# Second attention: where the gate is applied, and by which engine the projection is added to the rows

## The reference, cut to what matters

```
h = layernorm(x) * (1 + ca) + sa
Q, K, V = h @ Wq.T, h @ Wk.T, h @ Wv.T          # 16 heads of 16
scores = einsum('bshd,bstd->bsht', Q, K) / 4     # heads against heads, inside one token
attn = softmax(scores, axis=-1)
out = einsum('bsht,bstd->bshd', attn, V).reshape(b, s, dm)
x = x + ga * (out @ Wfc.T)                       # ga: one row of 256 per batch
h = layernorm(x) * (1 + cb) + sb                 # goes to the routed part
```

## Time and profile before

| what | value |
|---|---|
| median of 3 runs | 1049.5 us (1048.51 to 1049.79) |
| span of the profiled execution | 1045.7 us |
| second attention, first to last step | about 553 to 822 us of the span |
| busy over the span | PE 959.2 us, DVE 690.6 us, ACT 496.8 us, POOL 377.1 us |
| mean granted TensorE clock | 0.969 |

### The profile page before, as it was taken

One profiled execution on the slowest core, in us unless ns is written; L12 is line 12 of the kernel. 1 busy time (PEld: TensorE's weight loads), 2 busy tenths in 40 slices (PEclk: granted clock), 3 DMA queues, 4 the chain that ended last, 5 costly groups with the idle time before them and its releaser, 6 DMA issues. The chain is left out here.

```text
span 1045.7 us, 30362 instructions
## 1 busy us (share of the span) xinstructions
PE 959.2 (92%) x11177; PEld 823.6 (79%) x11178; DVE 690.6 (66%) x1747; ACT 496.8 (48%) x1343; POOL 377.1 (36%) x330
## 2 busy tenths in 40 slices
PE   6899999889999999999987999999767888999996
PEld 3466666879999999999965778888666878899995
DVE  3478877855777777777412688889985776344442
ACT  3556665404454554554446777777552440322221
POOL 0134335521223223222213455555561101455552
PEclk9999999999999999999998899999868999999998
DMA  9885581294232222221055657766421620444441
GB/s 338 216 331 122 126 269 41 97 386 115 85 102 79 87 97 85 89 92 71 8 107 92 115 124 150 154 134 128 99 68 57 266 108 22 151 134 140 134 136 35
DMA packets 133025, 135.59 MB, mean 130 GB/s; under 512 B 73884, under 2 KB 122142, under 8 KB 130740
## 3 DMA queue, kind: packets, MB, share of 16 engines
q1 hardware_dynamic: 121684, 90.80, 31.5%
q0 software_dynamic: 11232, 43.27, 13.0%
HBM read 96.21 MB, written 44.77 MB: 135 GB/s over the span
## 5 line engine op out<-in xcount | busy, mean ns | idle before, releaser
L1151 PE MATMUL psall<-rows 128*128 128x128 f32 x1872 | 224.8, 277 | 1.6 <-issue 1.1
L1151 PEld LDWEIGHTS psall<-rows 128*128 128x128 f32 x1872 | 219.6, 194 | 3.1 <-issue 1.3
L1114 POOL DMA_INDIRECT x<-ffn_rows,tok_i x78 | 82.6, 1059 | 171.8 <-DVE tok_i L999 69.9
L1165 PE MATMUL psall<-whi,rows 128*128 x624 | 141.0, 379 | 0.0
L1244 DVE COPY rows<-wlo 128x2048 f32 (+2 forms) x78 | 74.5, 955 | 95.8 <-PE psall L1151 85.2
L1165 PEld LDWEIGHTS psall<-whi,rows 128*128 128x128 f32 x624 | 115.7, 190 | 14.1
L1119 POOL DMA_INDIRECT attn_rows<-rows,tok_i x39 | 41.7, 1070 | 183.9 <-DVE rows L1276 183.9
L1504 DVE STREAM_TRANSPOSE whi<-whi 32x512 f32<-32x512 f32 x128 | 89.7, 701 | 9.1 <-POOL whi L1467 7.7
L1584 ACT ACTIVATE whi<-psall 32x512 f32<-32x512 f32 x128 | 75.3, 588 | 30.8 <-PE psall L1713 27.3
L280 PE MATMUL psall<-cst 128*128 128x128 f32 x714 | 88.4, 280 | 0.5 <-PEq L1387 0.5
L1306 ACT ACTIVATE rows<-psall,vs 128x128 f32<-128x128 f32 x312 | 85.0, 383 | 4.4 <-PE psall L1151 2.1
(11 more groups left out here) (250 smaller groups left out, 1731.3 us busy)
## 6 DMA issues: line engine op xcount, KB each, us to landing
ffn_rows<-mod_rows SPq DMA_DIRECT2D x2, 4096.0 KB
wlo<-in_W SPq DMA_DIRECT2D x2, 4096.0 KB, 17.5
whi<-in_w SPq DMA_DIRECT2D x5, 1024.0 KB
whi<-mod_rows SPq DMA_DIRECT2D x4, 1024.0 KB, 15.0
ffn_rows<-rows SPq DMA_DIRECT2D x8, 512.0 KB
ffn_rows<-x SPq DMA_DIRECT2D x8, 512.0 KB
wlo<-attn_rows SPq DMA_DIRECT2D x32, 128.0 KB, 3.4
v_turn<-wlo SPq DMA_DIRECT2D x32, 128.0 KB, 2.6
```

The costliest lines, as they stand in the source:

```text
L1114: eng.indirect_dma_start(xin[j % DEEP], None, src_d, bass.IndirectOffsetOnAxis(tok_i[:, j:j + 1].bitcast(U32), 0), bounds_check=T, oob_is_ ...
L1151: last = eng.matmul(b_up[t.par][f // 4][:, (f % 4) * P:(f % 4 + 1) * P], w_now[:, c, f * P:(f + 1) * P], inT[t.par][:, c * P:(c + 1) * P], ...
L1165: last = eng.matmul(b_dn[t.par][:, 0:D], hidT[t.par][:, f * P:(f + 1) * P], w_down[:, bass.ds(e, 1), f, :].rearrange("p o n -> p (o n)"), ...
```

## The change

The gate row is loaded by itself into one buffer (`gate_row`) at lag 14. GpSimd multiplies it into a copy of the projection's weights (`wfc_g`, 128x2048) in three parts of 768, 768 and 512 columns, in the first three of the four steps from lag 15 on, each at the end of GpSimd's list for that step. TensorE's projection reads `wfc_g` and waits for the third part. GpSimd's four additions per batch and VectorE's four gate multiplications are gone; VectorE adds the projection from PSUM to the rows of the whole batch in one instruction of 128x1024.

```diff
@@ constants and buffers
-        yb = cv(TB * D).rearrange("p (k d) -> p k d", d=D)
-        mod3 = [cw(3 * D).rearrange("p (j d) -> p j d", d=D) for _ in range(2)]
+        mod2 = [cw(2 * D).rearrange("p (j d) -> p j d", d=D) for _ in range(2)]
+        cx = Carve(x)
+        wfc_g = cx(HH * D).rearrange("p (j n) -> p j n", j=HH)
+        gate_row = cx(D)
+        b_y4 = psall[:, 0:TB * 512].rearrange("p (k n) -> p k n", k=TB)[:, :, 0:D]
@@ sync: layer_rows loads two rows, and
+                def load_gate(t):
+                    b = t // TB
+                    if t % TB == 0:
+                        eng.wait_ge(ev["pre"], 3 * B + b)
+                        eng.dma_start(gate_row, mod_d[b:b + 1, (6 + GA) * D:(7 + GA) * D].broadcast_to([P, D])).then_inc(s_wb, 16)
-                tile_steps([(0, load_norm), (LAG_VST, store_v), (LAG_VLD, load_v), (LAG_XLD, load_x), (LAG_ROW, layer_rows),
+                tile_steps([(0, load_norm), (LAG_VST, store_v), (LAG_VLD, load_v), (LAG_XLD, load_gate), (LAG_XLD, load_x), (LAG_ROW, layer_rows),
                             (LAG_H, store_rows), (LAG_QK, turn_k)])
@@ gpsimd
-                def add_attention(t):
-                    b, k = t // TB, t % TB
-                    eng.wait_ge(c_["ya"], b + 1)
-                    eng.wait_ge(s_x1[b % 2], 16 * (b // 2 + 1))
-                    eng.tensor_tensor(xr[b % 3][:, k, :], xr[b % 3][:, k, :], yb[:, k, :], ALU.add).then_inc(c_["xa"], 1)
-                tile_steps([(LAG_ET, normalize_exp), (LAG_X, add_attention), (LAG_MX, mask_other), (LAG_MX, sub_max)])
-                for t in LAST:
-                    add_attention(t)
+                def gate_weights(t):
+                    b, part = t // TB, t % TB
+                    if part == 0:
+                        eng.wait_ge(s_wa, 16 + 16 * (2 + TB))
+                        eng.wait_ge(s_wb, 48 + 16 * (b + 1))
+                        wait_some(eng, c_["y"], b)
+                    if part < 3:
+                        js = slice(3 * part, min(3 * part + 3, HH))
+                        last = eng.tensor_tensor(wfc_g[:, js], wfc[:, js], bc_mid(gate_row, js.stop - js.start), ALU.mult)
+                        if part == 2:
+                            last.then_inc(ev["pre"], 1)
+                tile_steps([(LAG_ET, normalize_exp), (LAG_MX, mask_other), (LAG_MX, sub_max), (LAG_Y, gate_weights)])
@@ vector
-                def gate_attention(t):
+                def add_attention(t):
                     b = t // TB
                     if t % TB == TB - 1:
                         eng.wait_ge(c_["y"], b + 1)
-                        eng.wait_ge(s_m3[b % 2], 48 * (b // 2 + 1))
-                        wait_some(eng, c_["xa"], TB * b)
-                        for k in range(TB):
-                            last = eng.tensor_tensor(yb[:, k, :], b_y[k], mod3[b % 2][:, 0, :], ALU.mult)
-                        last.then_inc(c_["ya"], 1)
+                        eng.wait_ge(s_x1[b % 2], 16 * (b // 2 + 1))
+                        eng.tensor_tensor(xr[b % 3], b_y4, xr[b % 3], ALU.add).then_inc(c_["xa"], 1)
@@ tensor: project
+                        eng.wait_ge(ev["pre"], 3 * B + t // TB + 1)
-                                last = eng.matmul(b_y[k], oT[at, j, :], wfc[at, j, :], start=j == 0, stop=j == HH - 1)
+                                last = eng.matmul(b_y[k], oT[at, j, :], wfc_g[at, j, :], start=j == 0, stop=j == HH - 1)
```

More of the change, by code:

```diff
@@ L1375, in done_by @@
             return min(max(t + lag - other - steps_ago + 1, 0), NT)
-        names = "nT hT v ve qk qke ss comp msk mx sub ex sm mul et pv oT y ya xa mv2 rs2 h tH h1T lg key"
+        names = "nT hT v ve qk qke ss comp msk mx sub ex sm mul et pv oT y xa mv2 rs2 h tH h1T lg key"
         c_ = {n: sem("c_" + n) for n in names.split()}
@@ L1433, in layer_rows @@
                         wait_some(eng, c_["h"], TB * (b - 1))
-                        for n, j in enumerate((GA, CB, SB_)):
-                            eng.dma_start(mod3[b % 2][:, n, :], mod_d[b:b + 1, (6 + j) * D:(7 + j) * D].broadcast_to([P, D])
+                        for n, j in enumerate((CB, SB_)):
+                            eng.dma_start(mod2[b % 2][:, n, :], mod_d[b:b + 1, (6 + j) * D:(7 + j) * D].broadcast_to([P, D])
                                           ).then_inc(s_m3[b % 2], 16)
+                def load_gate(t):
[3 more added lines that the diff above has]
+                        eng.dma_start(gate_row, mod_d[b:b + 1, (6 + GA) * D:(7 + GA) * D].broadcast_to([P, D])).then_inc(s_wb, 16)
                 def store_rows(t):
@@ L1510, in gate_attention @@
                         eng.wait_ge(c_["y"], b + 1)
-                        eng.wait_ge(s_m3[b % 2], 48 * (b // 2 + 1))
-                        wait_some(eng, c_["xa"], TB * b)
-                        for k in range(TB):
-                            last = eng.tensor_tensor(yb[:, k, :], b_y[k], mod3[b % 2][:, 0, :], ALU.mult)
-                        last.then_inc(c_["ya"], 1)
+                        eng.wait_ge(s_x1[b % 2], 16 * (b // 2 + 1))
+                        eng.tensor_tensor(xr[b % 3], b_y4, xr[b % 3], ALU.add).then_inc(c_["xa"], 1)
                 def stats_sum(t):
-                    eng.wait_ge(c_["xa"], t + 1)
+                    eng.wait_ge(c_["xa"], t // TB + 1)
                     ln = one_of(ln2, t)
@@ L1523, in norm2 @@
                 def norm2(t):
-                    m3 = mod3[t // TB % 2]
+                    m2 = mod2[t // TB % 2]
+                    eng.wait_ge(s_m3[t // TB % 2], 32 * (t // TB // 2 + 1))
                     h, (_, mean, rstd) = one_of(h1, t), one_of(ln2, t)
@@ L1529, in norm2 @@
                         wait_some(eng, s_hst[t % 2], t // 2, 16)
-                    ch.do(eng.scalar_tensor_tensor(h, xr[t // TB % 3][:, t % TB, :], mean[:, 0:1], m3[:, 1, :], ALU.subtract, ALU.mult))
-                    eng.scalar_tensor_tensor(h, h, rstd, m3[:, 2, :], ALU.mult, ALU.add).then_inc(c_["h"], 1)
+                    ch.do(eng.scalar_tensor_tensor(h, xr[t // TB % 3][:, t % TB, :], mean[:, 0:1], m2[:, 0, :], ALU.subtract, ALU.mult))
+                    eng.scalar_tensor_tensor(h, h, rstd, m2[:, 1, :], ALU.mult, ALU.add).then_inc(c_["h"], 1)
                 tile_steps([(LAG_H, norm2), (LAG_ET, turn_exp), (LAG_X, stats_sum), (LAG_MX, max_scores), (LAG_EX, sum_exp),
-                            (LAG_Y, gate_attention)])
+                            (LAG_Y, add_attention)])
                 norm2(FIRST_LAST - 1)
@@ L1708, in scores @@
                     wait_some(eng, c_["comp"], t)
-                    wait_some(eng, c_["ya"], done_by(t, LAG_S, LAG_Y) // TB)
+                    wait_some(eng, c_["xa"], done_by(t, LAG_S, LAG_Y) // TB)
                     for g in range(4):
```

## The result

| | before | changed |
|---|---|---|
| median of 4 runs | 1049.01 us (1046.14 to 1049.79) | 1078.32 us (1076.68 to 1080.21) |
| ratio | | 1.0286, 95% interval 1.0268 to 1.0304 |
| span of the profiled execution | 1045.7 us | 1074.8 us |

The change makes the kernel 2.9% slower; 1077.4 us were forecast, with 1064 to 1086 as the range. A second set of five runs of the same kernel on another chip gave 1079.30 us and a ratio of 1.0290 (1.0266 to 1.0315).

The account below looks back on a forecast made before the run. It took a 6.61 us ring between DVE and POOL as the bound; 3.5 + 19.1 + 3.7 + 2.6 - 1.0 = 27.9 us on a 1045.7 us span gave 1073.6, plus 3.8 made 1077.4 us, range 1064 to 1086.

Parts of the forecast that it names:

- batch 0: First batch, steps without norm2: all of each part shows, except 1.30 us of the first; 3.5 us more.
- batches 1 to 4: Batches whose three steps with parts pay in full: 4.91 - 0.14 = 4.77 us more each, 19.1 in all.
- batch 7: Last batch, no mask or subtraction left: the parts hide in POOL's 4.66 us idle before its last normalization, 0 added.
- the end: After the last batch: four POOL additions no longer stand before the last moments, 1.0 us off, between 0.1 and 3.1.
- The ring and its 0.2 us: Maximum, subtraction, normalization, transposes, moments, next maximum: closes in 6.61 us; POOL's normalization has 0.2 us to spare before DVE's transposes.
- The price of a part: POOL's multiplications between subtraction and normalization add 1.82 us per 768 columns, 1.27 per 512: 4.91 us a batch, low end 3.83.
- VectorE's gain: End of a batch: four gate instructions of 1.36 us become one addition of 1.225 us, 0.14 us less per batch.
- Batches 5 and 6: DVE's waits for the projection, 1.04 and 2.16 us, go first, so these batches add only 3.7 and 2.6 us.
- The new wait of the projection: TensorE's projection waits for the third part, but is done 2.4 us before DVE's addition is due: nothing lost at full clock.
- A: Rival: the parts fall into POOL's idle time and only the savings remain, 2 us less, 1047.5 us; chance 0.07.
- B: Rival: DVE's 2.08 us wait in each batch's first step takes part of the delay, 1065 us; chance 0.12.
- C: Rival: TensorE's clock falls and some steps with parts in four batches pay for it, +10 us, 1087 us; chance 0.10.

Follow-up runs that it names:

- the run with three matmuls: The changed kernel with 3 matmuls on constants ahead of TensorE's wait for norm2 in each step with a part: 1080.01 us, ratio 1.0298 to the kernel before.

## Why the prediction was right

| step of the prediction | forecast, us | measured, us |
|---|---|---|
| batch 0 | 3.5 | 2.9 at its mark; 3.7 from the first scores |
| batches 1 to 4 | 4 x 4.77 = 19.1 | 18.4 |
| batch 5 | 3.7 | 4.17 |
| batch 6 | 2.6 | 3.03 |
| batch 7 | 0 | 0.68 |
| the end | -1.0 | -0.08 |
| sum on the span | 27.9 | 29.1 |

*The ring and its 0.2 us.* Right, and shown from both sides: taken out of that place the parts cost nothing in batches 1 to 6, and the old additions put into it cost 12 us. A step with a part of 768 lasts 8.42 and 8.40 us from subtraction to subtraction, against 8.43 worked out; the stretch from subtraction to transposes is 4.25 against 4.26. The signs named in the prediction came: the idle time of the transposes behind the normalization (0.94 us), the second `norm2` instruction of 1.94 us, batches of 34.1 us. One did not: PE was to be busy 85% of a batch and was busy 93% (31.69 of 34.08 us), since its clock fell, which the sum had not counted on.

*The price of a part.* Of the two ends, 4.91 and 3.83 us a batch, the upper one was taken because `norm2` stood still behind the normalization. The trace has 2.02, 1.99 and 1.45 us for the parts beside `norm2`, and 1.82 and 1.26 in batch 0, where there is none. That is the exclusion of the Trainium skill ("SBUF — State Buffer", Who interferes with whom), and the trace agrees: with a part running, the second `norm2` instruction took 1.94 us instead of 0.48. Scaled from its figure for 2048 columns, the Trainium skill ("GPSIMD Engine Reference", Elementwise — side-by-side cycle accounting) gives an estimate of 1.69 us for a part of 768; here 1.82 was measured, so the line through the trace's 512 and 1024 columns was the better guide.

*VectorE's gain.* 0.20 us a batch, 1.36 to 1.16, where 0.14 was taken. That is about half of the 0.14 us by which the forecast of batches 2 to 4 was high; the other half is in the parts, whose three steps grew by 1.81, 1.79 and 1.24 us instead of 1.82, 1.82 and 1.27.

*Batches 5 and 6.* Here a step failed in size: "So the wait is gone". Of 1.04 and 2.16 us, 0.58 and 0.54 were left. The projection of batch 6 was not released by the third part (ends 806.21) but by ScalarE's copy, and it took 6.09 us where 5.54 was taken, since the clock was at half in more of it (mean 0.60 against 0.66 before). The rows: the projection, and the addition's remaining wait.

```profile
806.79 6.09 PE L1680 MATMUL psall<-x,whi 32*128 32x256 f32 x64 [2.55 <-ACT whi L1595]
...
812.95 1.23 DVE L1525 TENSOR_TENSOR wlo<-psall,wlo 128x1024 f32<-128x1024 f32 x1 [0.54 <-PE psall L1680]
```

*The new wait of the projection.* It was forecast at nothing, and in batches 1 to 7 nothing waits for a part. In batch 0 it did show: the projection started 2.18 us late behind the third part and took 5.42 us at a mean clock of 0.69. It ended at 608.53, when DVE had been ready for the addition since 608.45, so this cost 0.1 us at most.

```profile
603.11 5.42 PE L1680 MATMUL psall<-x,whi 32*128 32x256 f32 x64 [2.18 <-POOL x L1486]
```

*Batch 7.* "The parts hide there, 0" left out the exclusion that the same text had just counted: the first part runs from 813.62 to 815.44, and the first `norm2` instruction, issued at 814.09, takes 1.63 us instead of 0.48. The transposes then start 3.21 us after the mark instead of 2.60, which is nearly all of the 0.68 us.

```profile
813.62 1.82 POOL L1486 TENSOR_TENSOR x<-rows,x 128x768 f32<-128x768 f32 x1
...
814.09 1.63 DVE L1541 SCALAR_TENSOR_TENSOR rows<-wlo,small 128x256 f32<-128x256 f32 x1
```

*The end.* The first moments of the last batch come 2.05 us after the mark instead of 2.60, as hoped, but the last `norm2` starts its second half 9.50 us after it, before 9.57. In between DVE waits for ScalarE's deviations, 0.76 and 1.07 us after, 0.68 before. The gain became a wait for another engine.

```profile
842.55 0.48 DVE L1541 SCALAR_TENSOR_TENSOR rows<-wlo,small 128x256 f32<-128x256 f32 x1 [0.76 <-ACT small L1566]
...
846.63 0.48 DVE L1541 SCALAR_TENSOR_TENSOR rows<-wlo,small 128x256 f32<-128x256 f32 x1 [1.07 <-ACT small L1566]
```

*The rivals.* A (hidden in the idle time) describes the version with the parts ahead of the mask, not the change. B (DVE's wait in a batch's first step takes part of the delay) fell: that wait was 2.35 us after, not less. C (the clock) was right in that the clock fell, to 0.90 over batches 1 to 4, and wrong in its price: 0 in these batches, as the run with three matmuls showed.

*The time around the span.* The 3.8 us added to the span are two things. The profiled execution of the changed kernel took 1076.68 us with a span of 1074.8, so 1.9 us lie around a span; the other 1.9 were how far the profiled execution of the kernel before lay below the median of its runs. The changed kernel's lay 1.6 us below its own median, so the sum came out right by luck (3.8 against 3.5 us).

*How much is luck.* The forecast is 0.9 us off, and that is better than its terms. Batches 0 to 4 were forecast 1.3 us too high, the rest 2.5 us too low; for batch 0 that hangs on the attention's start, which lay 0.8 us earlier in the changed kernel's profile (552.21 against 552.99). The ring and its price are the larger part, 18.4 of 29.1 us in batches 1 to 4 alone, and these were right in mechanism and to 4% in size.

## What to carry to other kernels

An engine's idle share says nothing of whether it has room: find the stretch of the ring in which its next instruction is awaited, and how late that may be. GpSimd had 12 us idle in each batch and 0.2 us to spare at the end of its step; with the same three instructions the kernel was 29 us slower there, and 1.3 us slower, a ratio of 1.0015, one place further on. When work is added to an engine with a hand-written order, put it directly behind the instruction that others wait for, and in the start of the pipeline check again, as there the cover is another.

## What the runs showed of the hardware

Keeping TensorE's clock up was worth nothing where TensorE had idle time in each step: at a granted clock of 1.00 instead of 0.90 four batches kept their 34.1 us to within 0.02 us, and 2.05 us of filling matmuls a step made two batches over 1 us longer. It was worth 1.2 us in the one place where 24 filling instructions stood ahead of work that others waited for: 4.13 us at a mean clock of 0.67, 5.33 at 0.50.

A VectorE instruction with two inputs in SBUF stretched with what GpSimd was doing: the second `norm2` instruction took 0.48 us alone, 1.15 beside the normalization of 512 columns and 1.94 beside a part of 768, and ended 0.28 us after it. GpSimd paid less, some 0.2 us for each such instruction in front of its own (2.02 against 1.82 us, 1.23 against 1.05). The addition from PSUM took 1.16 us beside a normalization of 1.05, and the transposes 2.84 us beside a mask of 1.27; these neither slowed GpSimd nor were slowed.
